# Second attention of a two-layer kernel: the sine products of the rotary queries on GpSimd instead of VectorE, in 14 of 16 units

## The reference

```python
q_c = q @ W_dq                                   # 96 columns
q_rope = (q_c @ W_qr).reshape(b, lq, H, R)...    # 16 heads, R = 64
# _rope, with half = 32:
x1, x2 = (x[..., :half], x[..., half:])
return concatenate([x1 * cos - x2 * sin, x1 * sin + x2 * cos], axis=-1)
scores = (einsum('bhqd,bkhd->bhqk', q_nope, k_nope) + einsum('bhqr,bkr->bhqk', q_rope, k_rope)) * scale
scores = where(good, scores, NEG)
attn = softmax(scores, axis=-1)
out = einsum('bhqk,bkhd->bqhd', attn, v) ... @ W_o
```

## Time and the profile before

| | |
|---|---|
| median of 3 runs | 845.04 us (843.58 to 847.16) |
| span of the profiled execution | 841.8 us |
| busy PE, DVE, ACT, POOL over the span | 93%, 79%, 64%, 56% |
| stretch of the rotary queries (first sum to last) | 691.3 to 742.2 us |

### The profile page before, as it was taken

The page is one execution under the profiler, slowest core; times in us unless marked ns, Lnnn a source line. Parts: engine busy times, 40 slices in busy tenths (PEclk is TensorE's granted clock), DMA queues, the critical chain, the costliest instruction groups (busy, mean ns, idle before and its releaser), DMA issues.

```text
span 841.8 us, 14343 instructions
## 1 busy us (share of the span) xinstructions
PE 782.3 (93%) x4848; PEld 670.3 (80%) x4848; DVE 663.8 (79%) x1563; ACT 535.0 (64%) x1236; POOL 469.1 (56%) x786
## 2 busy tenths in 40 slices
PE   3687999999999999999899999999999999798998
PEld 2566788888888888888788878998888877577787
DVE  7789899899998989979889794865654589976634
ACT  6788877787778877788664555433332268974332
POOL 3688969779686895858855676442210015980000
PEclk9699999999999999999999999999999999999999
DMA  7000120011200121000200323967421010100001
GB/s 242 14 0 1 39 76 1 2 39 39 76 1 1 39 66 48 2 2 1 68 26 14 127 64 98 243 167 249 133 63 51 1 45 14 51 14 0 1 1 51
DMA packets 28265, 45.59 MB, mean 54 GB/s; under 512 B 3937, under 2 KB 18081, under 8 KB 28065
## 3 DMA queue, kind: packets, MB, share of 16 engines
q1 hardware_dynamic: 26800, 41.31, 17.0%
q10 hardware_dynamic: 1392, 3.37, 1.1%
HBM read 43.49 MB, written 1.18 MB: 53 GB/s over the span
## 4 chain that ended last, share of the span: by engine, by line
PE 59%; DVE 22%; ACT 11%; issue 5%; DMA 2%; POOL 1%; SPq 1%; ACTq 0%; DVEq 0%
PE PS L772 16%; PE PS L842 8%; PE PS L632 6%; PE PS L727 4%; PE PS L701 4%; PE PS L663 4%; PE PS L953 2%; PE PS L684 2%; PE PS L654 2%; PE PS L673 2%; DVE st L1638 2%; DVE yb L1540 2%; ACT P L1111 1%; PE PS L711 1%; DMA l_KM<-share 1%
## 5 line engine op out<-in xcount | busy, mean ns | idle before, releaser
L2222 POOL TENSOR_SCALAR raw<-raw,mvq,rsq 128x128 f32<-128x128 f32 x312 | 182.9, 600 | 1.6
L772 PE MATMUL PS<-xq,WH 128*128 128x512 f32 x472 | 148.5, 396 | 1.0 <-ACT l_x2T L997 1.0
L772 PEld LDWEIGHTS PS<-xq,WH 128*128 128x128 f32 x472 | 86.3, 190 | 18.1 <-issue 2.1
L632 PE MATMUL PS<-WH,xq 128*128 128x256 f32 (+1 forms) x256 | 88.7, 366 | 8.1 <-DVE xq L1544 8.1
L772 PE MATMUL PS<-xq,WL 128*128 128x512 f32 x236 | 92.5, 392 | 0.0
L632 PE MATMUL PS<-WL,xq 128*128 128x256 f32 (+1 forms) x256 | 84.5, 349 | 0.0
L1111 ACT ACTIVATE P<-PS,sm 128x256 f32<-128x256 f32 x128 | 61.0, 497 | 25.7 <-DVE sm L1702 25.6
L842 PE MATMUL PS<-xq,m_hh 128*128 128x256 f32 x384 | 69.9, 283 | 2.5 <-DVE m_hl L1998 1.2
L1638 DVE BATCH_NORM_STATS2 st<-raw 128x6 f32<-128x128 f32 x320 | 70.6, 277 | 1.5 <-ACT raw L1083 1.5
L701 PE MATMUL PS<-PT,vr 128*128 128x256 f32 x256 | 66.5, 382 | 4.7 <-ACT PT L997 4.7
L663 PE MATMUL PS<-kT,qT 128*128 128x256 f32 x256 | 65.9, 380 | 1.8 <-ACT qT L1100 1.8
(11 more groups left out here) (301 smaller groups left out, 2177.7 us busy)
## 6 DMA issues: line engine op xcount, KB each, us to landing
wst<-in_wgu SPq DMA_DIRECT2D x24, 256.0 KB, 4.0
l_KM<-share SPq DMA_DIRECT2D x16, 384.0 KB, 3.9
wst<-in_wall SPq DMA_DIRECT2D x18, 256.0 KB, 3.1
l_KM<-share SPq DMA_DIRECT2D x16, 256.0 KB, 5.2
dst<-in_wdn SPq DMA_DIRECT2D x24, 128.0 KB, 3.4
wst<-in_wkvx SPq DMA_DIRECT2D x8, 256.0 KB, 3.3
l_KM<-share SPq DMA_DIRECT2D x16, 128.0 KB, 4.4
m_pre<-in_wo ACTq DMA_DIRECT2D x1, 2048.0 KB, 10.2
```

The lines of the kernel that those rows point to most:

```text
L632: t = e.matmul(PS[:, b, o:o + n], xq[s][:, k, c * 128:(c + 1) * 128], W[:, k, w0:w0 + n], start=(k == 0 and i == 0), stop=(k == 1 and i == 1))
L772: t = e.matmul(PS[:, b, :], W[wi][:, gu, k, :], a[:, k, cols], start=(n == 0), stop=(n == 5))
L2222: t = e.tensor_scalar(v, v, mvq[:, par, n, 0:1], rsq[:, par, n:n + 1], ALU.add, ALU.mult)
```

## The change

The sine product moves from DVE to POOL in all units but (0, 0) and (0, 2). POOL waits for the swap itself, multiplies in place, waits for its own product, waits for the bank to be freed (that is, for DVE's cosine), and adds. DVE keeps all cosines and their waits.

```diff
+SINE_D = ((0, 0), (0, 2))
...
-        turned_q = count("turned_q", [(bb, u) for bb in range(4) for u in range(4)])
+        turned_q = count("turned_q", SINE_D)
...
                     w.wait_ge(swapped.sem, swapped.at[bb, u])
                     e.tensor_tensor(two[0], q, cos, ALU.mult).then_inc(free[b], 1)
-                    e.tensor_tensor(two[1], two[1], sin, ALU.mult).then_inc(turned_q.sem, 1)
+                    if (bb, u) in SINE_D:
+                        e.tensor_tensor(two[1], two[1], sin, ALU.mult).then_inc(turned_q.sem, 1)
...
                 for u in range(2 * part, 2 * part + 2):
                     n = 4 * bb + u
-                    w.wait_ge(turned_q.sem, turned_q.at[bb, u])
+                    if (bb, u) in SINE_D:
+                        w.wait_ge(turned_q.sem, turned_q.at[bb, u])
+                    else:
+                        v = tqs[n].rearrange("p (a t) -> p a t", a=2)
+                        w.wait_ge(swapped.sem, swapped.at[bb, u])
+                        e.tensor_tensor(v, v, tb_[:, 256:512].unsqueeze(1).to_broadcast([128, 2, 256]),
+                                        ALU.mult).then_inc(po.sem, 1)
+                        w.wait_ge(po.sem, po.up())
+                    w.emptied(("qr", bb, u))
                     e.tensor_tensor(QR[bb % 2][:, 2 * u:2 * u + 2, :].rearrange("p a b -> p (a b)"), tqc[n], tqs[n],
                                     ALU.add).then_inc(added.sem, 1)
```

## The result

The changed kernel takes 855.53 us (855.15 to 856.16, 4 runs) against 844.77 before: 1.012 times as long, 95% interval 1.0096 to 1.0146. Forecast were 848.5 us with a range up to 851.3. The direction was right; the size was not, by 7 us. The profiled span is 853.4 us for 841.8.

The account below looks back on a forecast made before the run. DVE bounds the chain until 731.69, then PE; the change puts a starved POOL queue on it. Walk +2.0 and clock +1.5 make +3.5: span 841.8 to 845.3, plus 3.2 to the median, 848.5 us; range 843.0 to 851.3.

Parts of the forecast that it names:

- Steps 1 to 3 of the walk: POOL's queue from its first sum: unit 5's sum and exps2(0) 2.4 us late, unit 11's sum 6.0 late.
- the walk: Engine queues followed with durations from the trace, from POOL's first sum past project(0): +2.0 us in sum.
- Step 4: From unit 11's sum through swap 13, soft(4) and turn_p(3) to project(0): it begins at 741.5 for 739.54.
- step 5: Behind project(0): POOL's part 7 ends at 750.7, scores(6) just covered, exps2(4) late by 7; nothing added.
- PE's clock, +1.5: Behind PE's 4.9 us wait for unit 11's sum, the clock falls to 1.2 GHz over matmuls: +1.5 us.
- late tail of POOL: POOL's pieces 6 to 8, ending at 762.6, hold DVE's path to 770: 1.3 to 2.5 us more; chance 0.30.
- DVE's relief comes through: DVE's relief counts and POOL keeps up: 843.7 us by the lower bound; chance 0.20.

Follow-up runs that it names:

- bank 6: Changed kernel with project(0) alone writing PSUM bank 6 in place of 7: 851.97 us, ratio 1.0077.
- tail wait: Changed kernel with POOL holding load_f's pieces 6 to 8 until DVE has ended the LayerNorm of add_l(0): 851.84 us, ratio 1.0078.
- pieces late: Changed kernel with pieces 1 to 8 of load_f all behind part 7's sums on POOL: 852.60 us, ratio 1.0076.
- sines from unit 6 with pieces late: Changed kernel with DVE making the sines of units 0 to 5, and load_f's pieces 1 to 8 behind part 7's sums: 850.36 us, ratio 1.0041.
- no product: Changed kernel without POOL's 14 products, those sine terms left out of the computation: 842.67 us, ratio 0.9966.
- sines from unit 6: Changed kernel with the change for units 6 to 15 alone, DVE making the sines of units 0 to 5: 850.73 us, ratio 1.0047.
- before with pieces late: Kernel before the change with pieces 1 to 8 of load_f behind part 7's sums: 855.06 us, ratio 1.0110.
- extra product: Kernel before the change, DVE making all sines, plus 14 unused products on POOL: 858.19 us, ratio 1.0139.
- pieces spread: Changed kernel, units 6 to 15 alone, load_f's pieces spread behind parts 3 to 7, pieces 7 and 8 waiting for add_l(0): 845.48 us, ratio 1.0015.

## Why the prediction was right or wrong

**What bounds.** Right: POOL, nearly full already, becomes the bound, and DVE's relief can't be used. The run without products shows that even free products would give 4.2 us at project(0), since ACT sets the pace then, and bank 7 holds project(0) for 1.0.

**Steps 1 to 3 of the walk.** Right to 0.1 us: the product at 1.27, unit 5's sum (13.1 us after the first), the wait of 1.8, unit 11's sum 40.2 for 40.3. The order of the queue, one duration for each kind of operation and the holds by L2091 were enough.

**Step 4 failed in its last clause.** It let project(0) follow turn_p(3). I had followed the data that each step needs, not the bank that project(0) writes. The time that step 5 gives part 7 puts unit 13's sum two units and piece 5 earlier: 750.7 - 2 x 2.58 - 2.63 = 742.9, 51.6 us after the first, measured 51.6. (The terms of the prediction give 749.8 for part 7; the 0.9 us more are not worked out there. A hold of 1.0 is in the trace: unit 13's product took 2.25 us for 1.27.) Swap 15 (1.3) and cosine 15 (0.8) behind it give 53.7; project(0) began at 53.8. So the number lay at hand, and step 5 put the lateness of that part aside: "nothing is added". With bank 6, where this link is cut, 51.9 was measured for the forecast's 51.7.

**PE's clock, +1.5.** It fell where I said (scores(4) took 2.08 for its 1.05, values 2.62 for 1.95), with a granted clock of 0.51 from 733.1 to 735.1, and it cost 1.7 us. It counts in the runs with bank 6. The wait ahead of it was shorter than forecast, 3.77 us for 4.9. In the changed kernel itself it counts nothing at that place, since the bank's chain through POOL is longer. A second fall, over turn_p(7) and project(2), cost 2.5 us; I hadn't asked what a longer wait there would do.

**The rival "late tail of POOL".** It held: the holds cost 1.5 us of the 1.3 to 2.5, and the tail wait brought them back. I had made it an alternative with a chance of 0.30, on the condition that POOL's last sum ends after about 748, though the walk itself had that sum end at 750.7: by its own condition it was part of the forecast. 3.7 us at project(0) without the bank's link (forecast: 3.5), 1.9 of the bank, 1.9 between project(1) and turn_p(7) (1.5 of them holds) and 2.5 of the second fall make the 10.0. The range was too narrow because losses that stand one behind the other on PE's path were set side by side.

**"DVE's relief comes through"** was rightly given little; even with another placing of POOL's pieces, fewer products and the other bank no gain clear of noise was measured (0.2%, interval up to none).

## What to carry to other kernels

When a late engine is followed to PE, the bank that the matmul writes belongs to the walk as well as the data it reads: ask of each of its first writes who emptied the place last, and what that one now waits for. Before moving elementwise work from VectorE to GpSimd, look at what VectorE does while GpSimd will be busy: a chain of small dependent SBUF operations was the dearest neighbour here (9.0 us for 3.1), since each of them can wait out a whole GpSimd operation, and holding GpSimd's work back until the chain has passed cost nothing here. Losses behind one another on the same path add, also those that one would rather call rivals.

## What the runs showed of the hardware that I had not expected

The holds strike operations of 128x2, of one input too: L1491, 0.17 us alone, took 0.87, and the LayerNorm from L1491 on, 14 operations, 9.0 for 3.1 us (pieces late). The batch statistics ahead of them (L1505, L1510) kept their 0.75 and 0.25 while POOL ran. The Trainium skill, SBUF — State Buffer, section "SBUF: two separate sides", names both kinds that compete with GpSimd, VectorE operations in a 2-port mode and those with two SBUF inputs; the rows agree for those with two inputs; in which mode the one-input L1491 ran, no row shows.

TensorE's clock fell to the 1.2 GHz level over turn_p(7) or project(2) in the runs where PE had waited for turn_p(7) 3.22 us (sines from unit 6 with pieces late), 3.41 (pieces late), 3.58 (no product), 3.98 (sines from unit 6), 4.07 (bank 6) and 4.08 (changed, both profiles, and before with pieces late). It did not where the wait was 2.43 (before), 2.69, 2.79, 2.81, 3.17 (extra product) or 3.39 (pieces spread). The two sets all but part by the wait before turn_p(7), but the length of a wait alone does not decide: project(0) of the extra-product run fell to 0.53 behind a wait of 2.76 us. Project(2) took 7.60 to 9.13 us in the first set for its 7.07, so a fall cost 0.5 to 2.1 us over it. The granted clock over the first 2 us behind turn_p(7)'s start was 0.50 in all of them but the run without products, where it fell only within project(2), to 0.56.
